# An encoder layer with routed experts on one core: GpSimd's order, paired tile transfers, scatters three to a slot, and expert tiles in every second slot

## The chip, the core and the metric

The kernel runs on one core of one Trainium2 chip. Engines are named as in the profile: PE is TensorE (PEld its weight load), DVE VectorE, ACT ScalarE, POOL GpSimd; SP is the sequencer that issues most DMAs. The metric is the device time of one execution in microseconds (us). Three runs of the kernel before have a median of 912.94 us (908.24 to 913.07).

## The reference

The input x has 64 sequences of 64 tokens with 128 features, the context the same shape. All arithmetic is float32. Cut to what matters:

```python
def _attn(q_in, k_in, v_in, wq, bq, wk, bk, wv, bv, wo, bo, causal):
    Q, K, V = ...                     # projections, 16 heads of 8
    scores = einsum('bqhd,bkhd->bhqk', Q, K) / sqrt(8)      # masked where causal
    return einsum('bhqk,bkhd->bqhd', softmax(scores), V).reshape(...) @ wo + bo

def _moe(x, rw, rb, w1, b1, w2, b2):                          # 8 experts, 128 -> 512 -> 128
    topw, topi = top_k(softmax(xf @ rw + rb), 2)
    combine = zeros.at[tokens, topi].add(softmax(topw))
    h = gelu(einsum('td,edf->etf', xf, w1) + b1)
    eo = einsum('etf,efd->etd', h, w2) + b2
    return einsum('etd,te->td', eo, combine)

x = _layernorm(x + _attn(x, x, x, ..., causal=True), ln1_g, ln1_b)
x = _layernorm(x + _attn(x, encoder_output, encoder_output, ..., causal=False), ln2_g, ln2_b)
x = _layernorm(x + _moe(x, ...), ln3_g, ln3_b)
```

## The kernel before

The 4096 tokens are 16 blocks of 256, each two tiles of 128 tokens. The program is one list of **slots** g, written out for every engine; each engine walks through the slots in order and does in slot g what stands there for it (the functions `slot(g)`), with semaphores between the engines. Slot g = 4t + s brings one attention **unit**, a tile of 128 tokens: for s = 0, 1 self attention of block t, for s = 2, 3 cross attention of block t - 2. A unit is spread over some seven slots: scores and row maxima in g, the two exponentials (the second, L749, gives the high parts) and the low parts (`probs_low`, shared by VectorE and GpSimd) in g + 1, the weighing in g + 2, output projection and residual in g + 3 (GpSimd's `spread` makes rstd there), VectorE's `norm` and GpSimd's `gain` in g + 4, the logits and the float16 halves of the result (`x2_high` on ScalarE, `x2_low` on GpSimd) in g + 5. Attention ends in slot 76.

The blocks are five **chunks** of 2, 3, 4, 4 and 3 blocks. When a chunk's units are done, VectorE routes it (slots 20, 32, 48, 64, 76 and the two behind each), GpSimd scatters its rows, sorted by expert, into a DRAM buffer `xs` (`scatter`, from slots 23, 35, 51, 67, 79, four indirect DMAs a slot), and the rows are worked off in **tiles** of 128 rows of one expert: 15, 19, 23, 23 and 19, together 99, numbered 0 to 98. TILE_SLOT says in which slot each stands. A tile needs its expert's weights (`load_tile_weights`, 512 KB, three tiles ahead, four buffers) and its rows (`load_tile_rows`, 64 KB, four tiles ahead, six buffers). PE turns the rows (`turn_tile`), multiplies up (`up`, 16 matmuls), ScalarE applies Gelu (L790), PE multiplies down (`down`, 9 matmuls), ScalarE copies y (`copy_y`) and SP stores it (`store_tile`). In each slot the first tile's step stands amid the attention work, further ones behind it: `for x in tiles[:1]: ...` and, at the end of the slot, `for x in tiles[1:]: ...`. In the slot before a chunk's first tile the chunk **opens**: SP issues three tiles' weights, waits for all scatters, and issues the first rows, and PE's last instruction of that slot turns them.

When a chunk's y is stored, GpSimd gathers for each block (a **group** f, at slot GROUP_SLOT[f]) the two picks of each token (`fetch_picks`, four indirect DMAs); VectorE sums and takes statistics two slots on (`gather_sum`), GpSimd makes rstd (`last_spread`, two slots on), VectorE normalizes (`final_norm`, three on) and GpSimd scales and stores to `out` (`last_gain`, three on). GpSimd's order in a slot is: x + bo, gain, x2_low, last_gain, last_spread, scatters, fetch_picks, probs_low, spread.

## Time and profile before

| what | value |
|---|---|
| median of 3 runs | 912.94 us |
| profiled execution: time, span | 903.71 us, 901.9 us |
| busy PE, PEld | 608.6 us (67%), 481.0 us (53%) |
| busy DVE, ACT, POOL | 475.6, 473.3, 388.2 us (53%, 52%, 43%) |
| granted clock of PE, mean | 0.851 of full speed |
| ACT_TABLE_LOAD | 92 of 1283 ns |
| POOL scatter L644, gather L658 | 64 of 1010 ns, 64 of 979 ns |
| POOL prob_lo L635, rstd L623, veps L621 | 979, 557, 224 ns each |
| POOL final_var_eps L664, frs L666 | 196, 717 ns each |
| DVE sums of picks with statistics (L1073, L1078, L1081, L1083) and final norm (L1092) | 12.5 + 12.3, 7.8, 2.5, 3.8 and 9.7 us for 16 groups |
| POOL waiting for x_hl (L629 on ACT L778) | 154.8 us in 32 times |
| PE waiting for a tile's rows (L1354 on xs) | 30.7 us in 5 times |

The first rows are shares of the whole span. Times "each" are means over all of a line's instructions, and an idle time in front of an instruction counts only where that engine holds up others. The kernel passes through stages of different kinds, so the rows further down are cut by stretches: attention alone (slots to 25), attention with tiles (26 to 71), tiles alone, and the end, in which GpSimd and VectorE finish the last chunk's blocks.

### The profile page before, as it was taken

How to read it: one execution, taken by the hardware profiler on the slowest of the kernel's cores; microseconds unless marked ns; L12 is line 12 of the kernel's file. 1: busy time of each engine (PE TensorE's matmuls, PEld its weight loads, DVE VectorE, ACT ScalarE, POOL GpSimd, SP SyncE). 2: the span in 40 equal slices, each digit the busy share in tenths (PEclk: the TensorE clock that was granted, in tenths of full speed). 3: DMA queues.
4: the chain of work that ended last, by engine and by line, in shares of the span. 5: the costliest groups of instructions: out<-in, count | busy, mean ns of one | idle time of the engine just before them, and what ended most of it. 6: DMA issues, size and time to landing. Idle time of an engine off the chain costs nothing. (4 is left out here: it accounts for less than half of the span.)

```text
span 901.9 us, 21537 instructions
## 1 busy us (share of the span) xinstructions
PE 608.6 (67%) x7898; PEld 481.0 (53%) x7898; DVE 475.6 (53%) x1319; ACT 473.3 (52%) x857; POOL 388.2 (43%) x611
## 2 busy tenths in 40 slices
PE   2677766666898785777877867787766766447800
PEld 1344444444776564665765646666555656446700
DVE  4468887575776754476785635665632144013021
ACT  1245454323899574686885856667626354123400
POOL 7133343235243461545235735354361466246064
PEclk9987897666999796898998879899976899778965
DMA  4625568235465425454554435535533566447710
GB/s 106 180 75 149 147 184 284 76 89 158 127 181 159 144 87 151 121 169 126 145 159 126 134 110 155 156 118 160 173 100 124 169 206 210 129 128 216 225 41 23
DMA packets 146024, 128.94 MB, mean 143 GB/s; under 512 B 14112, under 2 KB 127408, under 8 KB 145920
## 3 DMA queue, kind: packets, MB, share of 16 engines
q1 hardware_dynamic: 140864, 116.80, 43.7%
q0 software_dynamic: 5056, 10.76, 4.1%
q8 instruction: 64, 1.05, 0.5%
q14 instruction: 40, 0.33, 0.1%
HBM read 89.37 MB, written 40.24 MB: 144 GB/s over the span
## 5 line engine op out<-in xcount | busy, mean ns | idle before, releaser
L1384 PE MATMUL bank<-w_in,w_hl 128*128 128x128 f32 x792 | 126.9, 311 | 0.0
L921 DVE TENSOR_REDUCE row_max<-bank 128x16 bf16<-128x1024 f32 x64 | 78.2, 1222 | 87.0 <-PE bank L1266 78.1
L1384 PEld LDWEIGHTS bank<-w_in,w_hl 128*128 128x128 f32 x792 | 112.1, 219 | 0.4
L1314 PE MATMUL bank<-consts,o_n 128*128 128x64 f32 x256 | 47.1, 314 | 76.4 <-DVE o_n L940 64.4
L746 ACT ACTIVATE probT<-bank 128x1024 f32<-128x1024 f32 x64 | 65.5, 1024 | 60.0 <-PE bank L1290 34.5
L1373 PE MATMUL bank<-xT,w_in 128*128 128x128 f16 x1188 | 92.0, 231 | 4.1 <-issue 4.1
L658 POOL DMA_INDIRECT w_hl<-ys,pos x64 | 62.6, 979 | 72.5 <-DMA ys<-w_hl 54.5
L1314 PEld LDWEIGHTS bank<-consts,o_n 128*128 128x128 f32 x256 | 39.7, 220 | 90.2 <-issue 64.6
L790 ACT ACTIVATE w_hl<-bank 128x512 f32<-128x512 f32 x99 | 59.1, 597 | 54.7 <-PE bank L1373 34.6
L635 POOL TENSOR_TENSOR prob_lo<-probT,prob_hi 128x384 f16<-128x384 f32 x64 | 62.7, 979 | 51.2 <-ACT prob_hi L749 50.8
L1354 PE MATMUL bank<-ident_f,xs_tile 128*128 128x128 f16 x198 | 29.7, 235 | 79.9 <-ACT w_hl L798 39.2
L1373 PEld LDWEIGHTS bank<-xT,w_in 128*128 128x128 f16 x1188 | 78.9, 104 | 5.4 <-issue 5.4
L629 POOL TENSOR_TENSOR x_hl<-x_rows,x_hl 128x128 f16<-128x128 f32 x32 | 14.4, 451 | 154.8 <-ACT x_hl L778 154.8
L968 DVE TENSOR_SCALAR yn<-res,mv,rstd 128x128 f32<-128x128 f32 x64 | 25.7, 402 | 96.7 <-POOL rstd L623 96.2
L644 POOL DMA_INDIRECT xs<-x_hl,pos x64 | 64.6, 1010 | 18.8 <-issue 16.8
L914 DVE TENSOR_TENSOR prob_lo<-probT,prob_hi 128x640 f16<-128x640 f32 x64 | 57.1, 893 | 28.3 <-ACT prob_hi L749 28.3
L798 ACT ACTIVATE w_hl<-bank 128x128 f32<-128x128 f32 x99 | 27.3, 276 | 73.9 <-PE bank L1384 59.0
L1354 PEld LDWEIGHTS bank<-ident_f,xs_tile 128*128 128x128 f16 x198 | 12.5, 99 | 98.7 <-issue 66.7
L749 ACT ACTIVATE prob_hi<-bank 128x1024 f16<-128x1024 f32 x64 | 65.1, 1018 | 0.0
L783 ACT ACTIVATE xT<-bank 128x256 f16<-128x256 f16 x99 | 38.2, 386 | 46.7 <-PE bank L1354 43.4
L1290 PEld LDWEIGHTS bank<-q_st,k_all 128*64 128x64 f16 x2048 | 43.9, 125 | 34.4 <-issue 34.4
L1306 PE MATMUL bank<-v_hi,prob_hi 128*128 128x36 f16 x512 | 47.1, 181 | 20.4 <-issue 12.7
(149 smaller groups left out, 1606.4 us busy)
## 6 DMA issues: line engine op xcount, KB each, us to landing
...
k_all<-k_scr SPq DMA_DIRECT2D x128, 64.0 KB, 3.3
...
```

The lines of the kernel that those rows point to most:

```text
L635: pool.tensor_tensor(p_lo[u.buf][:, h, :], probT[u.buf][:, h, :], p_hi[u.buf][:, h, :], ALU.subtract).then_inc(lo_second[u.kind], 1)
L644: pool.indirect_dma_start(xs[c], bass.IndirectOffsetOnAxis(pos[c][:, k, t:t + 1], 0), x2_hl[:, n, :], None).then_inc(scattered[c], 16)
L658: pool.indirect_dma_start(got[f % 2][:, t, k, :], None, ys[c], bass.IndirectOffsetOnAxis(pos[c][:, k, n:n + 1], 0)).then_inc(got_in[f % 2] ...
L746: act.activation(probT[u.buf][:, :, :].rearrange("p h q -> p (h q)"), bank[:, KEYS:KEYS + 2, :].rearrange("p a n -> p (a n)"), ACT.Exp, sc ...
L749: act.activation(p_hi[u.buf][:, :, :].rearrange("p h q -> p (h q)"), bank[:, KEYS:KEYS + 2, :].rearrange("p a n -> p (a n)"), ACT.Exp, sca ...
L790: act.activation(hid[x.par][:, :, :].rearrange("p c t -> p (c t)"), bank[:, H_B, :], ACT.Gelu, scale=1 / W1_SCALE).then_inc(h_done, 1)
L914: dve.tensor_tensor(p_lo[u.buf][:, h, :], probT[u.buf][:, h, :], p_hi[u.buf][:, h, :], ALU.subtract).then_inc(lo_first[u.kind], 1)
L921: dve.reduce_max(row_max[u.buf][:, :], bank[:, SC:SC + 2, :].rearrange("p a (h k) -> p (a h) k", k=S), AX.X).then_inc(max_done[a], 1)
L1306: last = pe.matmul(bank[:, O_B, 36 * p:36 * p + 36], pt, v, start=k == 0, stop=k == 2, skip_group_check=True)
L1314: last = pe.matmul(turned_o[:, 64 * b:64 * b + 64], o_n[u.buf][:, b, :, :, :].rearrange("p c a d -> p (c a d)"), consts[:, C_DELTA:C_TRI], ...
L1373: last = pe.matmul(v[:, c * P:(c + 1) * P], w1_t[x.wb][:, i, c * P:(c + 1) * P], xT[x.par][:, j * P:(j + 1) * P], start=False, stop=True, ...
L1384: last = pe.matmul(expert_y, hid[x.par][:, c, :], w2_t[x.wb][:, c, :], start=False, stop=c == FC - 1, skip_group_check=True)
```

## The change

- `SCATTERS` is 3 a slot while attention runs, 8 behind it (before: 4).
- `TILE_SLOT`: while attention runs, a tile's slot is made odd (`g | 1`), so an even slot has no tile and an odd one two or three. The chunks' first tiles stand in slots 27, 41, 59, 75, 82 (before 26, 39, 56, 72, 83), so the chunks open in 26, 40, 58, 74 and 81.
- Groups of the first three chunks stand in every second slot: 42, 44; 60, 62, 64; 76, 78, 80, 82; then 83 to 86; 88, 89, 90 (before 40, 41; 57 to 59; 73 to 76; 84 to 87; 89 to 91).
- GpSimd's order in a slot is now: x + bo, gain, scatters, fetch_picks, last_spread, probs_low, spread, x2_low, last_gain; x2_low of a unit comes a slot later, last_spread three slots behind its fetch, last_gain five; VectorE's final_norm four. Small buffers of the final statistics are doubled.
- Rows and y of two tiles go in one DMA of 128 KB (`load_pair_rows`, `store_pair`; three buffers of pairs each). A pair is stored when the tile behind it is reached. The register read of a tile's weight row stands before the wait.

```diff
-SCATTERS = 4
+SCATTERS, LATE_SCATTERS = 3, 8
-WB, XB, YB = 4, 6, 4
+WB, XB, YB = 4, 3, 3
...
-        out += [g0 + i * n // TILES_OF[c] for i in range(TILES_OF[c])]
+        out += [g | 1 if (g := g0 + i * n // TILES_OF[c]) < ATTENTION_END else g for i in range(TILES_OF[c])]
...
-        g0 = max([TILE_SLOT[FIRST_TILE[c] + TILES_OF[c] - 1] + 2] + [out[-1] + 1 for _ in out[-1:]])
-        out += [g0 + i for i in range(CHUNK[c])]
+        step = 2 if MOE0[c] < ATTENTION_END - 4 else 1
+        g0 = max([TILE_SLOT[FIRST_TILE[c] + TILES_OF[c] - 1] + 1 + step] + [out[-1] + step for _ in out[-1:]])
+        out += [g0 + step * i for i in range(CHUNK[c])]
...
+                row = sp.value_load(tile_row[x.c][0:1, x.k:x.k + 1], min_val=0, max_val=(E - 1) * P)
                 if x.m >= WB:
                     sp.wait_ge(y_ready, x.m - WB + 1)
-                row = sp.value_load(tile_row[x.c][0:1, x.k:x.k + 1], min_val=0, max_val=(E - 1) * P)
...
+            def store_pair(x):
+
+                n = x.in_pair()
+                sp.wait_ge(y_done, x.m + n)
...
                 for x in tiles_in(g):
-                    if y := x.near(-2):
-                        store_tile(y)
-                    if y := x.near(XB - 2):
-                        load_tile_rows(y)
+                    if not x.half:
+                        if y := x.near(2 * XB - 2):
+                            load_pair_rows(y)
+                        if y := x.near(-2):
+                            store_pair(y)
                     if y := x.near(WB - 1):
                         load_tile_weights(y)
...
-                if (u := unit_at(g - 5)) and u.kind == CROSS:
-                    x2_low(u)
-                if (f := group_in(g - 3)) is not None:
-                    last_gain(f)
-                if (f := group_in(g - 2)) is not None:
-                    last_spread(f)
                 for c, n, k in scatters_at(g):
                     scatter(c, n, k)
                 if (f := group_in(g)) is not None:
                     fetch_picks(f)
+                if (f := group_in(g - 3)) is not None:
+                    last_spread(f)
                 if u := unit_at(g - 1):
                     probs_low(u)
                 if u := unit_at(g - 3):
                     spread(u)
+                if (u := unit_at(g - 6)) and u.kind == CROSS:
+                    x2_low(u)
+                if (f := group_in(g - 5)) is not None:
+                    last_gain(f)
...
-                if (f := group_in(g - 3)) is not None:
+                if (f := group_in(g - 4)) is not None:
                     final_norm(f)
```

How the instructions stand now, in three places. First GpSimd in slot 35, the first with scatters of the second chunk (yg and x_rows are the gain, x_hl is x2_low, xs the scatter). Before, the whole slot:

```order
L609 TENSOR_TENSOR yg<-yn,ln_g 128x128
L615 TENSOR_TENSOR x_rows<-yg,ln_b 128x128
L629 TENSOR_TENSOR x_hl<-x_rows,x_hl 128x128
L644 DMA xs<-x_hl,pos 2432x256 x4
L635 TENSOR_TENSOR prob_lo<-probT,prob_hi 128x384
L621 TENSOR_TENSOR veps<-mv,eps 128x1
L623 TENSOR_TENSOR rstd<-veps,minus_half 128x1
```

After, from the end of the gain in slot 35 to the end of slot 36:

```order
L640 TENSOR_TENSOR x_rows<-yg,ln_b 128x128
L669 DMA xs<-x_hl,pos 2432x256 x3
L660 TENSOR_TENSOR prob_lo<-probT,prob_hi 128x384
L646 TENSOR_TENSOR veps<-mv,eps 128x1
L648 TENSOR_TENSOR rstd<-veps,minus_half 128x1
L634 TENSOR_TENSOR yg<-yn,ln_g 128x128
L640 TENSOR_TENSOR x_rows<-yg,b_bo 128x128
L669 DMA xs<-x_hl,pos 2432x256 x3
L660 TENSOR_TENSOR prob_lo<-probT,prob_hi 128x384
L646 TENSOR_TENSOR veps<-mv,eps 128x1
L648 TENSOR_TENSOR rstd<-veps,minus_half 128x1
L654 TENSOR_TENSOR x_hl<-x_rows,x_hl 128x128
```

The scatters and the low part no longer have x_hl ahead of them: that unit's x_hl stands at the end of slot 36. Three scatters stand where four did.

Then ScalarE in attention with tiles (probT and prob_hi are the exponentials, w_hl<-bank 128x512 the Gelu, xT the copy of the turned rows). Before, one slot with a tile, up to the next one's exponentials:

```order
L746 ACT_TABLE_LOAD
L746 ACTIVATE probT<-bank 128x1024
L749 ACTIVATE prob_hi<-bank 128x1024
L783 ACTIVATE xT<-bank 128x256
L790 ACT_TABLE_LOAD
L790 ACTIVATE w_hl<-bank 128x512
L798 ACTIVATE w_hl<-bank 128x128
L725 ACTIVATE k_hl<-bank,bk 128x256
L737 ACTIVATE v_hi<-bank 64x2x16x8 x2
L778 ACTIVATE x_hl<-x_rows 128x128
L758 ACTIVATE oT<-bank 128x128
L772 ACTIVATE x_tile<-bank,ln_bc,ln_gc 128x128
```

After, from the exponentials of an even slot to the Gelu in the odd one behind it:

```order
L771 ACT_TABLE_LOAD
L771 ACTIVATE probT<-bank 128x1024
L774 ACTIVATE prob_hi<-bank 128x1024
L743 ACTIVATE inT<-bank 128x256 x2
L803 ACTIVATE x_hl<-x_rows 128x128
L783 ACTIVATE oT<-bank 128x128
L792 ACTIVATE x1T<-bank,ln_bc,ln_gc 128x128
L771 ACTIVATE probT<-bank 128x1024
L774 ACTIVATE prob_hi<-bank 128x1024
L808 ACTIVATE xT<-bank 128x256
L815 ACT_TABLE_LOAD
L815 ACTIVATE w_hl<-bank 128x512
```

Before, each slot has a table load ahead of the exponentials and one ahead of the Gelu; now the load for the exponentials stands in the even slot alone, the one for the Gelu in the odd. ACT_TABLE_LOAD stands 92 times in the program before and 58 times in this one.

Last GpSimd at the program's end, from the first gather of the last chunk's picks (w_hl<-ys,pos) on. Before:

```order
L658 DMA w_hl<-ys,pos 128x128 x4
L672 TENSOR_TENSOR w_hl<-w_hl,ln_g 128x256
L675 TENSOR_TENSOR w_hl<-w_hl,ln_b 128x256
L678 DMA out<-w_hl 128x2x128
L658 DMA w_hl<-ys,pos 128x128 x4
L664 TENSOR_TENSOR final_var_eps<-fmv,eps 128x2
L666 TENSOR_TENSOR frs<-final_var_eps,minus_half 128x2
L658 DMA w_hl<-ys,pos 128x128 x4
L672 TENSOR_TENSOR w_hl<-w_hl,ln_g 128x256
L675 TENSOR_TENSOR w_hl<-w_hl,ln_b 128x256
L678 DMA out<-w_hl 128x2x128
```

After:

```order
L683 DMA w_hl<-ys,pos 128x128 x4
L689 TENSOR_TENSOR final_var_eps<-fmv,eps 128x2
L691 TENSOR_TENSOR frs<-final_var_eps,minus_half 128x2
L697 TENSOR_TENSOR w_hl<-w_hl,ln_g 128x256
L700 TENSOR_TENSOR w_hl<-w_hl,ln_b 128x256
L703 DMA out<-w_hl 128x2x128
L683 DMA w_hl<-ys,pos 128x128 x4
L689 TENSOR_TENSOR final_var_eps<-fmv,eps 128x2
L691 TENSOR_TENSOR frs<-final_var_eps,minus_half 128x2
L697 TENSOR_TENSOR w_hl<-w_hl,ln_g 128x256
L700 TENSOR_TENSOR w_hl<-w_hl,ln_b 128x256
L703 DMA out<-w_hl 128x2x128
```

Behind the first gather there now stand a spread and a gain of the chunk before, and so behind the second one and, for the gain, the third. From there to the end come seven gains with stores to `out` and five spreads, where there were four and three.

## Rows read from the trace of the kernel before

**Rows 1.** Stretches: start:end length, busy us of each engine (instructions), PEclk, DMA share, GB/s

```profile
111.36:132.51 21.15, 13.55 (x228) 9.86 (x224) 17.70 (x45) 11.73 (x24) 9.64 (x19) 1.00 0.65 186
235.84:274.40 38.56, 34.47 (x553) 27.48 (x550) 29.22 (x74) 36.44 (x62) 15.04 (x28) 1.00 0.61 174
274.40:284.07 9.67, 8.11 (x115) 6.19 (x111) 5.06 (x16) 8.00 (x16) 3.60 (x8) 1.00 0.37 112
356.37:366.79 10.42, 9.17 (x142) 7.50 (x141) 6.63 (x17) 8.58 (x16) 2.92 (x6) 0.99 0.41 123
```

**Rows 2.** Timeline of ScalarE in slot 31: start us, us, engine, line, operation

```profile
264.32 1.28 ACT L746 ACT_TABLE_LOAD   x1
...
267.85 1.28 ACT L790 ACT_TABLE_LOAD   x1
269.14 0.60 ACT L790 ACTIVATE w_hl<-bank 128x512 f32<-128x512 f32 x1
```

**Rows 3.** Timeline of TensorE, end of slot 32 and start of 33; in brackets idle before, releaser

```profile
280.47 0.55 PE L1314 MATMUL bank<-consts,o_n 128*128 128x64 f32 x3 [0.37 <-ACT w_hl L798]
```

**Rows 4.** Timeline of GpSimd in slot 35

```profile
308.57 0.60 POOL L629 TENSOR_TENSOR x_hl<-x_rows,x_hl 128x128 f16<-128x128 f32 x1 [1.33 <-ACT x_hl L778]
...
315.37 0.57 POOL L623 TENSOR_TENSOR rstd<-veps,minus_half 128x1 f32<-128x1 f32 x1
```

**Rows 5.** Stretches between second exponentials of named slots

```profile
190.22:225.29 35.07, 24.71 (x249) 16.11 (x250) 19.95 (x54) 11.21 (x23) 18.41 (x28) 0.60 0.42 126
...
302.89:336.29 33.40, 26.05 (x335) 19.72 (x333) 19.28 (x56) 21.56 (x38) 20.93 (x30) 0.85 0.34 100
336.29:356.37 20.08, 9.56 (x104) 7.42 (x102) 7.33 (x17) 7.57 (x15) 4.12 (x8) 0.67 0.53 157
366.79:446.17 79.38, 62.58 (x894) 50.31 (x892) 52.91 (x139) 59.31 (x100) 37.83 (x64) 0.91 0.50 146
472.47:515.35 42.88, 34.45 (x451) 26.91 (x450) 25.59 (x71) 29.24 (x49) 28.54 (x39) 0.84 0.41 122
515.35:531.91 16.56, 9.43 (x103) 7.16 (x102) 6.37 (x17) 7.88 (x15) 3.81 (x8) 0.69 0.42 127
543.61:599.80 56.19, 42.18 (x568) 34.20 (x566) 36.32 (x100) 37.46 (x63) 27.30 (x44) 0.88 0.50 146
619.86:693.89 74.03, 49.54 (x599) 41.33 (x596) 30.34 (x101) 40.39 (x74) 29.69 (x44) 0.82 0.44 133
693.89:861.68 167.79, 109.36 (x1200) 100.03 (x1197) 36.57 (x150) 61.69 (x141) 71.50 (x93) 0.89 0.58 177
```

**Rows 6.** Timelines of SP's DMA queue and of TensorE in slot 38

```profile
340.42 2.64 SPq L487 DMA_DIRECT2D w_in<-w_scr  x3
...
348.46 0.40 PE L1354 MATMUL bank<-ident_f,xs_tile 128*128 128x128 f16 x2 [9.24 <-DMA xs_tile<-xs]
```

**Rows 7.** Timeline of ScalarE: Gelu (L790) of tiles 57, 79, 80, 88 and 89

```profile
696.50 0.60 ACT L790 ACTIVATE w_hl<-bank 128x512 f32<-128x512 f32 x1
...
783.84 0.60 ACT L790 ACTIVATE w_hl<-bank 128x512 f32<-128x512 f32 x1 [0.62 <-PE bank L1373]
...
797.26 0.60 ACT L790 ACTIVATE w_hl<-bank 128x512 f32<-128x512 f32 x1 [1.20 <-PE bank L1373]
...
829.77 0.60 ACT L790 ACTIVATE w_hl<-bank 128x512 f32<-128x512 f32 x1 [0.53 <-PE bank L1373]
...
832.41 0.60 ACT L790 ACTIVATE w_hl<-bank 128x512 f32<-128x512 f32 x1 [0.53 <-PE bank L1373]
```

**Rows 8.** Timeline of GpSimd at the program's end

```profile
861.68 1.05 POOL L658 DMA_INDIRECT w_hl<-ys,pos  x1 [30.29 <-DMA ys<-w_hl]
...
866.56 0.74 POOL L672 TENSOR_TENSOR w_hl<-w_hl,ln_g 128x256 f32<-128x256 f32 x1
...
868.40 0.81 POOL L678 DMA_DIRECT2D out<-w_hl  x1 [0.29 <-POOL w_hl L675]
...
891.13 0.76 POOL L678 DMA_DIRECT2D out<-w_hl  x1 [0.30 <-POOL w_hl L675]
```

More of the change, by code:

```diff
@@ L132, with scatters_in @@
 SCATTER = [r + 3 for r in ROUTE]
-MOE0 = [SCATTER[c] + -(-2 * NT[c] // SCATTERS) + 1 for c in range(CHUNKS)]
 ATTENTION_END = last_cross(CHUNKS - 1) + 6
+def scatters_in(slot):
+    return SCATTERS if slot < ATTENTION_END else LATE_SCATTERS
+MOE0 = [SCATTER[c] + -(-2 * NT[c] // scatters_in(SCATTER[c])) + 1 for c in range(CHUNKS)]
 TAIL_RATE = 4
@@ L159, in __init__, with in_pair @@
         self.first, self.last = self.k == 0, self.k == TILES_OF[self.c] - 1
-        self.par, self.wb, self.xb, self.yb = m % 2, m % WB, m % XB, m % YB
+        self.par, self.wb = m % 2, m % WB
+        self.half = self.k % 2
+        self.pair = FIRST_PAIR[self.c] + self.k // 2
+        self.xb, self.yb = self.pair % XB, self.pair % YB
+    def in_pair(self):
+        return 1 if self.last else 2
     def near(self, d):
         return Tile(self.m + d) if 0 <= self.k + d < TILES_OF[self.c] else None
+LAST_OF = {Tile(m).pair: m for m in range(NMOE)}
 def tiles_in(slot):
@@ L399, in uses_of @@
         def uses_of(k, c):
-            return sum(m % YB == k for m in range(FIRST_TILE[c] + TILES_OF[c]))
+            return sum(p % YB == k for p in range((FIRST_PAIR + [Tile(NMOE - 1).pair + 1])[c + 1]))
         @blk.sync
@@ L549, in slot @@
                     sp.wait_ge(cleared, 16 * CHUNKS)
-                    for d in range(XB - 2):
-                        load_tile_rows(x.near(d))
+                    for d in range(XB - 1):
+                        load_pair_rows(x.near(2 * d))
             load_tokens(SELF, Block(0))
@@ L1347, in turn_tile @@
             def turn_tile(x):
[L1349 removed]
+                pe.wait_ge(xs_in[x.xb], 16 * (x.pair // XB + 1))
                 if x.m == 0:
```

60 lines of the change are left out of this document (32 added, 28 removed).

## Prediction

> **What bounds the kernel now.** I read the stretches first, then ScalarE's timeline in a quiet place, then GpSimd's in a disturbed one. The second exponential (L749) runs once a slot, so its starts give every slot's length; the stretches are cut at them. In three quiet slots without an expert tile a slot takes 21.15 / 3 = 7.05 us, with VectorE busy 17.7 of 21.15: the round of maxima, low parts, o_n and back through TensorE. In five quiet slots with one tile each it takes 38.56 / 5 = 7.7 us, with ScalarE busy 36.4 of 38.56; a slot with two takes 9.7 or, where more projections stand in it, 10.4 [rows 1]. ScalarE is full there because each slot loads the table of Exp and the table of Gelu, 1.28 us each [rows 2]. So one tile hides nearly whole (+0.65), a second hardly: it stands at the slot's end, PE begins the next slot's L1314 only at 280.47, after the copy of the second tile's result, some 2.5 us late [rows 3].
>
> That is the quiet pace. Slots 26 to 63 hold 46 tiles, eight slots with two; at 7.7 and 10.0 (between 9.7 and 10.4) they would need 30 x 7.7 + 8 x 10.0 = 311 us. Three things stand on top. In slots with scatters GpSimd waits for ScalarE's x_hl, then issues four indirect transfers of 1.3 us, and only then makes the low probabilities and rstd, on which VectorE's normalization waits [rows 4]. In slots that gather picks the same happens. And where a chunk opens, PE stands for its first rows [rows 6]. The rest is read from the stretches [rows 5]. Slots 35 to 37 take 33.4 us, 10.3 over the pace; slots 51 to 54 take 42.9, 12.1 over; slots 23 to 25 take 35.1. The picks cost 79.4 - 63.9 = 15.5 and 56.2 - 43.1 = 13.1. The openings in slots 38 and 55 take 20.1 and 16.6, so 12.4 and 8.9 over.
>
> **The change part by part.**
>
> *GpSimd's order and three scatters a slot.* x2_low no longer stands before the scatters and the low probabilities. GpSimd's round in a scatter slot becomes normalization 0.5, gain 1.0, three scatters 3.8, low part 0.95, rstd 1.0, x2_low 0.45 and the handovers: about 8.0 (durations from the table above). In a slot without tiles that is 1 us over 7.05; in one with two or three tiles it hides. Slots 23 to 56 have 13 scatter slots after the change, 8 of them without tiles: 8 us, where slots 23, 24, 35 to 37 and 51 to 54 now lose 9.7 + 10.3 + 12.1 = 32 (slots 23 and 24 begin at 190.22 and take 23.85 of the 35.07). **-24.**
>
> *Picks in every second slot.* Five fetches fall into slots without tiles: four gathers of 1.27 make GpSimd's round about 9, +2 each; five sums with their normalization, 48.6 / 16 = 3.0 us each by the table above, fall on VectorE, which has 1.15 us a slot free there: +1.9 each. Some 19 for 28.6 now. **-10.**
>
> *Tiles in the second of two slots.* ScalarE saves 34 table loads of 92, 34 x 1.28 = 43.5 us of work. What that is worth is read from the pace: a pair now costs 2 x 7.7 = 15.4, and then 7.05 + 10.0 = 17.05, as ScalarE stops being the bound and the serial second tile takes its place. Slots 26 to 63 become 19 x 7.05 + 14 x 10.0 + 5 x 12.7 (three tiles, one more 2.64) = 337.5 for 311. **+26.** The bounds: if every load saved were time, -43.5; if the two-tile slots take 10.4 and the empty ones are no shorter than a slot with one tile, 14 x 0.4 + 19 x 0.65 = 18 more, +44. I take the middle of the measured slots.
>
> On the table switch the row says that Gelu starts at 269.14, right behind a load of 1.28 us from 267.85 [rows 2]. The Trainium skill (ScalarE: Activation LUTs, What ACT_TABLE_LOAD costs) gives 1283 ns for the load, which the row confirms, and 1380 ns of drain on top, which it does not show. By the page 34 switches would be worth 90 us and the advice to group by table set would decide the case; by the rows they are worth 43.5 at most.
>
> *Openings.* The first chunk now opens in slot 26, the second in 40, the third in 58. SP there must send and fetch q and k (26, 58), or wait for PE's turn of the tokens and then send k (40), before it issues three weight tiles and the rows; rows reach PE 8 us after the first weight issue (340.42 to 348.46) [rows 6]. In slot 38 the first weight issue stands 4.1 us behind the second exponentials (340.42 to 336.29) and the slot takes 20.1, with 2.1 of the old chunk's last tile in it: 18, less 7.7 is 10, which I take for 58. In 26 the slot before has no tile, so the exponentials come earlier and SP's sends do not: I put 4 more; in 40 PE's turn of the tokens stands before the send: 3 more. Both are choices between 0 and the 8 us that the load takes. That is 14 + 13 + 10 = 37, for 4.2 (slot 25, 35.07 - 23.85 - 7.05) + 12.4 + 8.9 = 25.5 now. Two paired loads for four shorten SP's issue by 0.9 us. **+9** after rounding down for that.
>
> The paired transfers do nothing else: the rows' four issues take 1.77 us and PE's waits for rows are those of the openings. The Trainium skill (DMA: Bandwidth & Descriptors, Rules for kernel authors) says to coalesce many small transfers into large ones; its fixed cost of about 2 us (stated for the GpSimd path) would, as an estimate, save 4 us at each of five openings, and the time would be 922. The row has the rows land behind three weight tiles of 512 KB, which pairing leaves alone.
>
> *Slots 64 to 71*, 74.0 us now [rows 5]: -3, since the fourth opening leaves them and scatters stand three to a slot.
>
> Attention together: -24 - 10 + 26 + 9 - 3 = **-2.**
>
> *The fourth chunk.* It now opens in slot 74 with no attention left to cover it. Now its first Gelu runs 2.6 us after the last exponentials (693.89 to 696.50). After the change come two tiles of the third chunk in slot 73 and its last down projection in 74, some 12 us, then an opening as bare as the fifth chunk's is now: 797.26 - 783.84 = 13.4 us from Gelu to Gelu [rows 7]. That is 25 for 2.6: +22. The 42 tiles behind it need 2.64 each at best (829.77 to 832.41), 111 us of the 167.8 [rows 5, 7]; less of attention's finish stands between them, -4. **+18.**
>
> *The end.* Now GpSimd waits until 861.68 for the last rows of y and then issues three groups' gathers (5.0 each), four gains with their stores (2.7 each, 866.56 to the end of the store at 869.21) and three spreads (1.0 each, by the table above), and issues the last store at 891.13 [rows 8]: 30.2 us. After the change the last three gains of chunk four and two of its spreads stand behind the first gather of chunk five in GpSimd's order. They have been ready for long, but GpSimd sits in the wait. That is 3 x 2.7 + 2 x 1.0 = 10 us; normalizations that wait for out stores just issued (landing some 2 us later, an estimate from the 8.0 us that three weight tiles and a tile's rows take [rows 6]) add about 3. **+13.**
>
> The sum is -2 + 18 + 13 = +29 us. On the profiled execution, 903.7 us (span 901.9), that is 933; that execution is 9.2 us under the median of the three runs, 912.9. The measured time should stand to the median: **942 us**.
>
> **The rivals.**
>
> *Faster (14%).* ScalarE's saved loads come through as time: the tile's second step overlaps the following empty slot, since that slot's PE has 7.6 of 21.15 us free [rows 1]. A pair then costs 14.1 in place of 17.05, 19 pairs give -56, and the sum is about -27: 886 us. For it: ScalarE is nearly full now. Against it: the two-tile slots in the trace are already longer by the whole second step.
>
> *No change (9%).* Fewer stalls keep PE's clock up: it is granted 0.60 in slots 23 to 25 and 0.67 in the opening slot, against 1.00 where it is quiet [rows 1, 5]. If that gives 10 us, and the bare opening costs half of what I say and the sum for pairs 10 less, I am at 913.
>
> *Much slower (12%).* Loads of weights wait behind indirect transfers, which now come in the same slots as nothing else, and 3-tile slots ask 1.5 MB at once; each of the nine three-tile slots then loses 2 us more, and the empty slots take 7.7: +18 and +12, 972 us.
>
> *The change does not do what it says*: pairing and spreading move no bound and GpSimd's wait for x_hl was idle anyway. Without the -24 the time is 966; it shares the 12% of the case before.
>
> **How the numbers follow.** My forecast, 925 to 960, has 65%. The range reaches from 908, which takes in most of the unchanged case, to 964; it leaves out the faster case and half of the slowest. What a measurement can tell from no change is 0.5%, 4.6 us. Faster 14% and a little of the lower edge, 0.15; same 0.09; slower 0.76.
>
> **What would show it.** Right: 58 table loads; no GpSimd wait for x_hl before scatters; starts of the second exponentials alternating near 7 and 10; a PE stall of 7 to 10 us for rows behind slots 26, 40, 58 and 74; about 43 us from GpSimd's first gather of the last chunk to its last store. Wrong: pairs near 15 us, or the fourth chunk's gains done before that gather. The attention part up to the last exponentials should end at 692, within 15 us; if it ends at 660, the term for the pairs is wrong.

## The result, and the profile after

The changed kernel takes 966.4 us (median of 4 runs, 966.2 to 972.9) against 910.6 (903.6 to 913.1): a ratio of 1.066, 95% interval 1.061 to 1.070. It is slower, as forecast, but by 56 us and not by 29. The profiled execution takes 966.2 us with a span of 964.4, 62.5 over the span before. Cut at the second exponentials (now L774), with the kernel of e1 beside it, which is the changed one with its tiles one to a slot. Slots 26 to 63 hold 46 tiles before, 43 after and in e1:

| stretch, us | before | after | e1 | forecast for the change |
|---|---|---|---|---|
| up to slot 23 | 190.2 | 199.0 | 191.2 | 0 |
| slots 23 to 25 | 35.1 | 28.4 | 27.6 | |
| slots 26 to 63 | 394.6 | 427.1 | 375.9 | with the row above and below: -2 |
| slots 64 to 71 | 74.0 | 73.0 | 70.6 | |
| last exponentials to last copy of y | 165.1 | 181.6 | 182.8 | +18 |
| last copy of y to last store | 32.1 | 44.4 | 44.4 | +13 |

The stretches of after, in the form of [rows 1, 5]: slots 10 to 19; 23 to 25; 26 to 63; then slots 28, 30, 31 (two tiles), 32, 33 (three tiles), and 28 to 31 together.

```profile
core 0: us, PE busy (x) PEld busy (x) DVE busy (x) ACT busy (x) POOL busy (x), PEclk, DMA share, GB/s
83.28:165.31 82.03, 57.24 (x775) 39.30 (x771) 62.90 (x145) 38.41 (x74) 28.03 (x49) 0.79 0.61 184
199.04:227.43 28.39, 19.70 (x268) 13.12 (x269) 20.37 (x55) 10.81 (x22) 18.22 (x27) 0.76 0.26 75
227.43:654.50 427.07, 307.64 (x4242) 236.25 (x4238) 250.00 (x660) 240.79 (x439) 173.45 (x278) 0.86 0.43 129
256.71:265.68 8.97, 5.93 (x60) 3.36 (x58) 5.03 (x13) 3.40 (x8) 2.99 (x6) 0.70 0.33 95
277.30:284.11 6.81, 4.67 (x56) 3.11 (x55) 5.18 (x16) 3.64 (x8) 3.21 (x5) 0.76 0.57 164
284.11:295.47 11.36, 9.95 (x162) 8.42 (x161) 7.38 (x17) 8.87 (x18) 2.57 (x5) 1.00 0.47 146
295.47:304.45 8.98, 5.93 (x59) 3.36 (x57) 5.32 (x15) 3.41 (x9) 2.99 (x6) 0.63 0.33 96
304.45:320.17 15.72, 12.60 (x201) 10.77 (x202) 9.57 (x31) 12.24 (x21) 3.65 (x7) 0.99 0.39 114
256.71:295.47 38.76, 31.52 (x440) 23.97 (x437) 24.11 (x59) 24.20 (x46) 12.42 (x23) 0.87 0.43 131
```

The last second exponential starts at 727.5 us; the forecast had 692, within 15.

ScalarE did save what the change was made for: it is busy 240.8 us in slots 26 to 63 (284.2 before, 280.4 in e1), and the whole program has 58 table loads. But none of the three prices of the forecast for a pair stands. A quiet slot with two tiles takes 11.4 us (10.0 forecast), one with three 15.1 to 15.7 (12.7), and a slot without tiles 5.9 to 9.0 (7.05), mostly at a granted clock of 0.63 to 0.76. Slots 28 to 31 hold four tiles in 38.8 us.

What fills a two-tile slot is in ScalarE's and PE's timeline of slot 31. The second tile's xT copy (289.74) stands behind k_hl, v_hi and x_hl; PE waits 1.04 us for it, and o_n, which VectorE has ready at 288.5, is turned (L1341) only at 291.80.

```profile
287.37 0.28 ACT L823 ACTIVATE w_hl<-bank 128x128 f32<-128x128 f32 x1
288.25 0.47 ACT L750 ACTIVATE k_hl<-bank,bk 128x256 f16<-128x256 f32 x1 [0.60 <-PE bank L1274]
288.62 0.76 ACT L762 ACTIVATE v_hi<-bank 64x256 f16<-64x256 f32 x2
289.40 0.31 ACT L803 ACTIVATE x_hl<-x_rows 128x128 f16<-128x128 f32 x1
289.74 0.38 ACT L808 ACTIVATE xT<-bank 128x256 f16<-128x256 f16 x1
290.02 0.59 ACT L815 ACTIVATE w_hl<-bank 128x512 f32<-128x512 f32 x1
```

```profile
288.39 0.83 PE L1400 MATMUL bank<-xT,w_in 128*128 128x128 f16 x12
290.26 0.22 PE L1408 MATMUL bank<-b_all,chosen_biases 128*128 128x128 f16 x1 [1.04 <-ACT xT L808]
290.32 1.11 PE L1411 MATMUL bank<-w_in,w_hl 128*128 128x128 f32 x8
291.80 0.66 PE L1341 MATMUL bank<-consts,o_n 128*128 128x64 f32 x4 [0.37 <-ACT w_hl L823]
```

Slot 47 has two tiles in both kernels, the same copies between them and a granted clock of 1.00. It takes 10.7 us before and 11.2 after, where a slot without a tile stands in front of it. PE's share in it is larger: before, PE has weighed just as the second exponential starts; after, it weighs 1.0 to 1.6 us behind that start. First before, then after:

```profile
435.48:446.22 10.74, 8.52 (x114) 6.70 (x111) 5.73 (x17) 8.76 (x18) 2.92 (x6) 1.00 0.62 175
```

```profile
462.11:473.27 11.16, 9.75 (x160) 8.22 (x158) 7.64 (x20) 8.76 (x17) 7.16 (x12) 1.00 0.45 128
```

The tail is as forecast. The fourth chunk's first Gelu runs 26.0 us behind the last exponentials (25 forecast, 2.6 before), and PE waited for its rows; ScalarE's rows:

```profile
727.54 1.02 ACT L774 ACTIVATE prob_hi<-bank 128x1024 f16<-128x1024 f32 x1
...
753.53 0.60 ACT L815 ACTIVATE w_hl<-bank 128x512 f32<-128x512 f32 x1 [1.35 <-PE bank L1400]
```

So is the end: GpSimd's timeline from the first gather of the last chunk to the last store, 41.8 us (29.5 before [rows 8]). Spreads and gains of chunk four stand between the gathers (here the first such pair).

```profile
911.83 1.03 POOL L683 DMA_INDIRECT w_hl<-ys,pos  x1 [28.92 <-DMA ys<-w_hl]
...
916.66 0.20 POOL L689 TENSOR_TENSOR final_var_eps<-fmv,eps 128x2 f32<-128x2 f32 x1
916.94 0.72 POOL L691 TENSOR_TENSOR frs<-final_var_eps,minus_half 128x2 f32<-128x2 f32 x1
917.65 0.71 POOL L697 TENSOR_TENSOR w_hl<-w_hl,ln_g 128x256 f32<-128x256 f32 x1
...
933.18 1.04 POOL L683 DMA_INDIRECT w_hl<-ys,pos  x1 [4.18 <-DVE w_hl L1100]
...
953.59 0.75 POOL L703 DMA_DIRECT2D out<-w_hl  x1 [0.29 <-POOL w_hl L700]
```

### The profile page after: what moved, and what is told of

Read it like the earlier page. It is cut to its first block and busy times, and to the rows that moved or that the text cites. A ratio compares the mean times of both kernels' runs of the same rounds, so it can differ in the third digit from the quotient of the medians.

```text
span 964.4 us, 21371 instructions
## 1 busy us (share of the span) xinstructions
PE 619.0 (64%) x7898; PEld 480.0 (50%) x7898; DVE 482.3 (50%) x1319; ACT 433.1 (45%) x823; POOL 395.5 (41%) x611
## 5 line engine op out<-in xcount | busy, mean ns | idle before, releaser
L946 DVE TENSOR_REDUCE row_max<-bank 128x16 bf16<-128x1024 f32 x64 | 78.3, 1224 | 190.2 <-PE bank L1293 162.4
L660 POOL TENSOR_TENSOR prob_lo<-probT,prob_hi 128x384 f16<-128x384 f32 x64 | 67.4, 1053 | 157.6 <-ACT prob_hi L774 156.8
L1341 PE MATMUL bank<-consts,o_n 128*128 128x64 f32 x256 | 51.1, 334 | 109.4 <-DVE o_n L965 90.9
L1411 PE MATMUL bank<-w_in,w_hl 128*128 128x128 f32 x792 | 115.8, 291 | 0.0
L1341 PEld LDWEIGHTS bank<-consts,o_n 128*128 128x128 f32 x256 | 42.3, 235 | 122.7 <-issue 105.8
L1411 PEld LDWEIGHTS bank<-w_in,w_hl 128*128 128x128 f32 x792 | 101.6, 200 | 0.7 <-issue 0.2
L646 POOL TENSOR_TENSOR veps<-mv,eps 128x1 f32<-128x1 f32 x64 | 14.4, 226 | 176.7 <-DVE mv L984 176.7
L939 DVE TENSOR_TENSOR prob_lo<-probT,prob_hi 128x640 f16<-128x640 f32 x64 | 67.0, 1047 | 31.8 <-ACT prob_hi L774 31.7
L1400 PEld LDWEIGHTS bank<-xT,w_in 128*128 128x128 f16 x1188 | 78.4, 104 | 0.0
L1119 DVE TENSOR_SCALAR w_hl<-w_hl,fmv,frs 128x128 f32<-128x128 f32 x32 | 13.4, 460 | 123.1 <-POOL frs L691 58.7
L783 ACT ACTIVATE oT<-bank 128x128 f32<-128x128 f32 x64 | 17.8, 278 | 113.5 <-PE bank L1354 88.6
L1317 PEld LDWEIGHTS bank<-q_st,k_all 128*64 128x64 f16 x2048 | 47.7, 132 | 39.5 <-issue 39.5
L774 ACT ACTIVATE prob_hi<-bank 128x1024 f16<-128x1024 f32 x64 | 65.1, 1017 | 0.0
L1305 PE MATMUL bank<-max_diag,consts_bf 128*128 128x512 bf16 x128 | 51.4, 491 | 8.4 <-DVE max_diag L951 8.4
```

The source lines that it names most:

```text
L660: pool.tensor_tensor(p_lo[u.buf][:, h, :], probT[u.buf][:, h, :], p_hi[u.buf][:, h, :], ALU.subtract).then_inc(lo_second[u.kind], 1)
L774: act.activation(p_hi[u.buf][:, :, :].rearrange("p h q -> p (h q)"), bank[:, KEYS:KEYS + 2, :].rearrange("p a n -> p (a n)"), ACT.Exp, sca ...
L939: dve.tensor_tensor(p_lo[u.buf][:, h, :], probT[u.buf][:, h, :], p_hi[u.buf][:, h, :], ALU.subtract).then_inc(lo_first[u.kind], 1)
L946: dve.reduce_max(row_max[u.buf][:, :], bank[:, SC:SC + 2, :].rearrange("p a (h k) -> p (a h) k", k=S), AX.X).then_inc(max_done[a], 1)
L1305: pe.matmul(bank[:, KEYS + n, :], ones_bf, max_diag[u.buf][:, 4 * n:4 * n + 4, :, :].rearrange("p a q c -> p a c q"), start=True, stop=True)
L1341: last = pe.matmul(turned_o[:, 64 * b:64 * b + 64], o_n[u.buf][:, b, :, :, :].rearrange("p c a d -> p (c a d)"), consts[:, C_DELTA:C_TRI], ...
```

## The experiments

All results, as ratios to the kernel before on the same chip. Runs of different lines stood partly on different chips (medians of before: 907.1 to 914.2), so ratios are compared, not medians. Ratios move from chip to chip too: the same kernel has 1.055 in e14 and 1.064 in e18. A difference of 1% between runs on different chips is therefore not settled by the table. The stretch is slots 26 to 63 of the profiled execution; it holds 46 tiles in the kernel before, e2 and e4, 41 in e3, 44 in e10 and e12, and 43 in the others. The same code differs there from profile to profile: 422.7 to 428.8 us for the changed kernel with either kind of transfer, 375.9 and 370.0 in e1 and e7.

| run | median us | ratio (95% interval) | 26 to 63 |
|---|---|---|---|
| changed kernel | 966.4 | 1.066 (1.061 to 1.070) | 427.1 |
| e1 tiles one to a slot | 909.5 | 0.999 (0.995 to 1.004) | 375.9 |
| e2 before, tiles in odd slots | 958.8 | 1.049 (1.041 to 1.057) | 436.1 |
| e3 changed, even slots | 979.6 | 1.072 (1.064 to 1.081) | 415.7 |
| e5 changed, filler | 951.9 | 1.051 (1.045 to 1.056) | 409.3 |
| e6 changed, second step earlier | 961.7 | 1.061 (1.056 to 1.065) | 422.0 |
| e4 before, x2_low late | 912.6 | 1.001 (0.996 to 1.006) | 399.9 |
| e8 before, three scatters | 915.2 | none (runs of 903.4 to 921.6 us) | 395.1 |
| e9 e1, single transfers | 898.0 | 0.989 (0.985 to 0.992) | 368.4 |
| e15 e9, groups each slot | 917.6 | 1.006 (1.002 to 1.009) | 377.6 |
| e16 e9, x2_low early | 913.9 | 1.002 (0.997 to 1.006) | 376.3 |
| e7 e1, gains first | 902.9 | 0.997 (0.994 to 0.999) | 370.0 |
| e10 e7, chunk 4 opens sooner | 910.3 | 1.010 (1.005 to 1.016) | 383.9 |
| e11 e7, early filler | 893.4 | 0.985 (0.983 to 0.988) | 375.3 |
| e12 e10, early filler | 902.2 | 0.997 (0.994 to 1.001) | 382.4 |
| e13 e9, gains first, early filler | 894.2 | 0.979 (0.973 to 0.984) | 371.7 |
| e14 changed, single transfers | 967.9 | 1.055 (1.049 to 1.060) | 427.6 |
| e17 changed kernel again | 970.3 | 1.065 (1.058 to 1.072) | 428.8 |
| e18 e14 again, beside e17 | 965.8 | 1.064 (1.058 to 1.069) | 422.7 |

### What the pairs of slots cost: e1 and e2

```diff
-        out += [g | 1 if (g := g0 + i * n // TILES_OF[c]) < ATTENTION_END else g for i in range(TILES_OF[c])]
+        out += [g0 + i * n // TILES_OF[c] for i in range(TILES_OF[c])]
```

> The changed kernel with its tiles spread one to a slot as before; order of GpSimd, paired transfers, three scatters and groups in every second slot stay. Theory P (the pairs of slots cost, because a second tile's step stands serially at the end of an odd slot): slots 26 to 63, 427.1 us in the changed kernel, fall by 26 to 35 us, the last second exponential comes near 695, and the whole is 930 to 940 us. Rival O (the new order of GpSimd and the openings cost, the pairs are free): 26 to 63 fall by less than 8 us and the whole stays over 955. In both, slots 1 to 22 stay as long as in the changed kernel (start of slot 23 at 199).

e2 is the same line the other way round, in the kernel before.

> The kernel before with one edit: a tile's slot is made odd while attention runs. Theory P: two-tile slots take 11 to 11.5 us, empty ones 7 to 7.5, so slots 26 to 63 (394.6 us before) grow by 20 to 35 and the whole is 930 to 945 us. Rival (the 34 saved table loads come through as time): 870 to 900 us. Rival O (the pairs are free): 905 to 918 us.

The pairs of slots are the whole slowdown: without them the changed kernel is level with the one before, and alone they cost 1.049. In slots 26 to 63 they cost 51.2 us from e1 and 41.5 from the kernel before, more than either theory had put down, and both medians fell outside every range given. Slot 23 of e1 starts at 191.2 and not at 199. Slots 28 to 31 of e1, four tiles one to a slot, at full clock, take 31.1 us where the changed kernel takes 38.8:

```profile
247.58:278.64 31.06, 27.92 (x455) 22.46 (x453) 25.25 (x60) 28.84 (x50) 13.49 (x23) 1.00 0.56 164
```

### Where the second step stands: e3 and e6

e3 rounds the slot up to an even one (`g + g % 2` for `g | 1`).

> The changed kernel with its tiles in even slots in place of odd ones (a slot's number rounded up). Theory K (the odd slots are the bad hosts: in them ScalarE copies key and value, 0.47 and 0.76 us, between the two Gelus, and the two-tile slot takes 11.4 us where an even one took 9.7): two-tile slots of s = 0 take 9.7 to 10.2 us, and the whole is 945 to 958 us. Rival (which of the two slots makes no difference; the second step costs the same anywhere): 962 to 972 us.

e6 moves the second tile's step, on both engines:

```diff
+                early = 2 if g < ATTENTION_END else 1
-                for x in tiles[:1]:
+                for x in tiles[:early]:
                     tile_step(x)
...
+                for x in tiles[1:early]:
+                    ...
                 if s == 0 and (sa.exists() or ca.exists()):
```

> The changed kernel with the second tile's step placed ahead of the projections on TensorE and ahead of their copies on ScalarE, while attention runs. Theory K (the second step's xT copy waits behind ScalarE's 0.94 to 1.23 us of key, query and value copies, and its matmuls behind 1.0 us of projections, and the two-tile slot takes 11.4 for it): two-tile slots take 10 to 10.4 us, 19 slots give 20 us, the whole is 942 to 952 us. Rival (the work is the same and only its order differs): 960 to 970 us.

Neither run bears K out in size. In e3 quiet two-tile slots of s = 0 take 10.7 and 10.3 us (9.7 to 10.2 expected), those of s = 2 11.4 and 10.5, and the whole missed both ranges. Its chunks open a slot later and more of its groups stand at the end (last copy of y to last store: 53.2 us); e3 doesn't separate the two. In e6 slot 31 takes 11.0 instead of 11.4, and the whole stays in the rival's range: a gain of 0.4 to 0.5%, which the intervals don't tell from none. The work has only changed places: now ScalarE waits 0.45 and 0.53 us inside the second step, which nothing covers, and k_hl and v_hi stand ahead of oT instead.

```profile
282.65 0.38 ACT L808 ACTIVATE xT<-bank 128x256 f16<-128x256 f16 x1 [0.45 <-PE bank L1382]
283.56 0.60 ACT L815 ACTIVATE w_hl<-bank 128x512 f32<-128x512 f32 x1 [0.53 <-PE bank L1401]
...
285.44 0.47 ACT L750 ACTIVATE k_hl<-bank,bk 128x256 f16<-128x256 f32 x1 [0.60 <-PE bank L1275]
285.82 0.76 ACT L762 ACTIVATE v_hi<-bank 64x256 f16<-64x256 f32 x2
286.60 0.31 ACT L803 ACTIVATE x_hl<-x_rows 128x128 f16<-128x128 f32 x1
286.94 0.28 ACT L783 ACTIVATE oT<-bank 128x128 f32<-128x128 f32 x1
```

### What the empty slots cost: e5

```diff
+            def filler(g, n):
+                if MOE0[0] <= g < ATTENTION_END and not tiles_in(g):
+                    ...
+                    for k in range(n):
+                        pe.matmul(bank[:, H_B, (k % 4) * P:(k % 4 + 1) * P], ident_h[:, :], ident_h[:, :], ...)
```

> The changed kernel with filler work on TensorE: in every slot without a tile, 12 and at its end 16 matmuls of 128 columns into the bank that holds Gelu's input, whose result nobody reads. Theory G (the slots without a tile are long because TensorE's granted clock falls in them, 0.70 on the mean of 19 such slots against 0.98 in the two-tile slots): their granted clock rises to 0.9 or more, the quiet ones go from about 7.9 to 7.1 us, and the whole falls by 8 to 15 us, 951 to 958 us. Rival S (the serial second and third step are all of it): the 28 matmuls cost or are hidden, the whole is 964 to 985 us.

Adding work made the kernel 1.4% faster, by the ratios of e5 and e17 too, which stood on one chip; the whole is in theory G's range. Slots 28, 30 and 32 take 7.2, 5.9 and 7.2 us for 9.0, 6.8 and 9.0, at a granted clock of 1.00; over the 19 slots without a tile the clock goes from 0.70 to 0.85 and the mean length from 9.7 to 8.5.

```profile
254.16:261.38 7.22, 5.70 (x100) 4.25 (x99) 5.04 (x13) 3.42 (x9) 2.98 (x6) 1.00 0.31 89
271.90:277.76 5.86, 5.29 (x99) 4.43 (x96) 5.58 (x16) 3.68 (x8) 2.69 (x4) 1.00 0.55 154
288.59:295.81 7.22, 5.70 (x100) 4.25 (x99) 5.33 (x15) 3.42 (x9) 2.98 (x6) 1.00 0.32 90
```

So of the 51 us some 18 are the clock (427.1 - 409.3): a mean of 0.70 says that PE ran its share of the attention round partly at 1.2 GHz and not at 2.4, and with the filler slots 26 to 63 as a whole have the granted clock of e1, 0.91. This also shows what a quiet pair costs at full clock. Slots 28 to 31, two pairs, take 34.4 us, 17.2 a pair, for the 17.05 of the forecast and 19.4 in the changed kernel; slots 32 and 33, none and three tiles, take 22.4 for 19.75:

```profile
254.16:288.59 34.43, 30.39 (x491) 24.97 (x491) 24.61 (x59) 24.01 (x45) 12.61 (x23) 1.00 0.50 146
288.59:310.98 22.39, 17.75 (x286) 14.64 (x286) 15.52 (x46) 15.64 (x28) 6.63 (x13) 1.00 0.41 125
```

The other 33 us I put down to the second and third steps behind which the round waits, as in slot 31; that is what is left over, and no run takes them away.

### GpSimd's order, scatters and groups: e4, e8, e15, e16

e4: in the kernel before, x2_low moves to the end of the slot, at `g - 6`. e8: in the kernel before, `SCATTERS, LATE_SCATTERS = 3, 8`. e15: e9 with `step = 1`. e16: e9 with x2_low at `g - 5` ahead of the scatters.

> The kernel before with one edit: GpSimd's x2_low comes a slot later and last in the slot. Theory X (the 8.8 us that slots 5 to 22 lose in the changed kernel come from this: GpSimd's low probabilities now always run beside VectorE's max_diag, 1.36 for 0.69 us, and TensorE's granted clock falls to 0.7): slot 23 starts at 197 to 200; the scatter slots gain about 10, so the whole is 905 to 915 us. Rival C (the loss of slots 5 to 22 is a clock that differs from run to run): slot 23 starts at 189 to 192 and the whole is 893 to 905 us.

> The kernel before with one edit: three scatters a slot while attention runs and eight behind it, so that the chunks open in slots 26, 39, 57, 73, 81. Theory A (of the 29 us that slots 23 to 71 gain in e1, the three scatters a slot give 15 to 20): the last second exponential at 674 to 681 for 693.9, the tail 15 to 18 longer because the fourth chunk opens bare: 905 to 915 us. Rival (GpSimd's order gives them; three scatters alone leave slots 23 to 71 within 6 us): 920 to 932 us.

> e9 with the groups of picks in slots that follow each other (41, 42; 59, 60, 61; 75 to 78). Theory (my term for picks: a group every second slot is worth 10 us in slots 26 to 63): those slots take 376 to 382 us for 368.4, the whole is 905 to 912 us. Rival (the spacing moves nothing): 895 to 902 us.

> e9 with x2_low a slot earlier and ahead of the scatters again, as before the change. Theory (GpSimd's order is worth most of what is left of the 24 us term, in the scatter slots): slots 23 to 63 longer by 8 to 16 us, the whole 905 to 914 us. Rival (e4 and e8 say that neither the order nor the three scatters alone does anything; then the final statistics' staging does it): 895 to 902 us.

Alone, neither brings a gain of the whole. The late x2_low leaves slots 23 to 71 where they were (504.2 us for 503.7). The three scatters shorten them by 6.9 us, 5.3 of it in slots 23 to 25, and make the last exponentials to the last y 15.1 us longer, since the fourth chunk then opens bare; e8's two theories had 15 to 20 and under 6 for the first part, so neither is right.

Taken out of e9, the spacing of the groups costs 1.7% in all (9.2 us in slots 26 to 63) and the place of x2_low 1.3% (7.9 us there, 3.7 in slots 23 to 25), but e15 and e16 ran on another chip than e9. On their own chip stands e13, which has the same code in slots 27 to 63 and takes 371.7 us in 26 to 63: against it the spacing is worth 5.9 us there and the place of x2_low 4.6, no more than e1 and e7 differ by. In the whole, e15 and e16 are 2.8 and 2.4% behind e13. Its early filler (0.9 to 1.3%, e12 and e11) and its gains ahead of the fetch (0.3% by the ratios of e7 and e1, 0.9% by the 8 us of the end) account for 1.2 to 2.2% of that, which leaves, as an estimate, 0.6 to 1.6% for the spacing and 0.2 to 1.2% for x2_low. So both probably help, and x2_low's worth is hardly clear of noise. e16 fell in its theory's range, e15 (917.6) over both of its ranges. What the three scatters bring among the other parts, no run shows.

Theory X holds in part (e4's slot 23 starts at 194.8 us, between the two ranges). Slots 10 to 19 hold no tile and no scatter in any kernel. Over all profiled executions they take 75.2 to 78.4 us in the four kernels with x2_low early and 78.0 to 83.5 in the thirteen others without early filler: some 4 us for the place, as much again from run to run. Both go with the clock: before, and e7 (x2_low late):

```profile
81.03:156.23 75.20, 51.01 (x776) 36.43 (x772) 61.85 (x145) 38.43 (x73) 27.68 (x49) 0.89 0.67 200
```

```profile
83.26:166.78 83.52, 59.52 (x776) 40.84 (x771) 62.88 (x145) 38.42 (x73) 28.28 (x50) 0.76 0.62 185
```

What x2_low's move does there is seen in slots 15, 16 and 19, where x2_low stood in front: GpSimd's prob_lo no longer waits for ScalarE's x_hl and starts 2 to 4 us sooner. In slot 15 it then starts beside VectorE's max_diag, which takes 1.36 us. In the kernel before it took 0.69 there with GpSimd waiting (the 1.36 is found in the kernel before too, in slot 18, so it comes from the meeting and not from the new order alone). First after, VectorE and GpSimd, then before:

```profile
126.53 1.36 DVE L951 TENSOR_TENSOR max_diag<-consts_bf,row_max 128x1024 bf16<-128x1024 bf16 x1
...
126.43 0.91 POOL L660 TENSOR_TENSOR prob_lo<-probT,prob_hi 128x384 f16<-128x384 f32 x1 [1.23 <-ACT prob_hi L774]
```

```profile
119.68 0.69 DVE L926 TENSOR_TENSOR max_diag<-consts_bf,row_max 128x1024 bf16<-128x1024 bf16 x1
...
121.83 0.91 POOL L635 TENSOR_TENSOR prob_lo<-probT,prob_hi 128x384 f16<-128x384 f32 x1
```

The Trainium skill (SBUF — State Buffer, Who interferes with whom) says that a VectorE instruction with two SBUF inputs and a GpSimd instruction that reads SBUF block each other for a whole instruction. The rows nearly agree: prob_lo starts first, and max_diag ends 0.55 us behind its end, where alone it takes 0.69.

### The transfers: e9, e14, e17, e18

```diff
-WB, XB, YB = 4, 3, 3
+WB, XB, YB = 4, 6, 4
-        self.half = self.k % 2
-        self.pair = FIRST_PAIR[self.c] + self.k // 2
+        self.half = 0
+        self.pair = m
```

> The kernel of e1 with rows and y of each tile in a transfer of their own again. Theory (pairing moves nothing, since rows are waited for only behind an opening's weights): 905 to 914 us, slots 26 to 63 within 5 us of e1's 375.9. Rival (pairing is worth what the skill's rule on coalescing gives, or SP's shorter list is what made slots 26 to 63 fast): 918 to 930 us.

> The changed kernel with one transfer a tile for rows and y; its tiles stay in odd slots. Theory Q (pairing itself costs about 10 us, all of it at the five openings: the last but one y store of a chunk waits for the second y of its pair ahead of the next chunk's weights in SP's order, and the first rows are 128 KB): 953 to 960 us, the first Gelus of chunks four and five 2 to 4 us nearer to the tile before. Rival (e9's gain came from something that one tile a slot brings, or is the spread between chips): 963 to 970 us.

> The changed kernel once more, so that it stands on the same chip as e18: 962 to 974 us. Its slots 1 to 22 are the second look at the early loss: theory C (a granted clock that differs from run to run) lets slot 23 start anywhere from 190 to 200, a cost of the change would put it at 199 again.

> The kernel of e14, beside e17. If pairing costs 1% in the changed kernel, as the ratios to before say (1.0656 and 1.0547, taken on different chips), this is 8 to 11 us under e17. If the medians of e14 and of the changed kernel (967.9 and 966.4) tell it rightly, within 3 us of e17.

Across chips single transfers looked 1% faster twice (e9, e14). On one chip the changed kernel with pairs has 1.065 and without 1.064: no difference that can be told, and e18 is 4.5 us under e17, between its two cases; e14 fell in its rival's range. The openings differ by little: slot 58 takes 14.9 and 14.9 us in e14 and e18 for 17.3 and 16.8, the fifth chunk's first Gelu comes 14.2 and 14.2 us behind the last of the fourth for 15.9 and 16.2; the fourth chunk's goes the other way (17.7 and 18.2 for 16.6 and 17.0). The four openings behind the first, from a chunk's last Gelu to the next one's first, add up to 89.3 and 88.9 us with pairs and 85.7 and 86.6 without.

With one tile a slot theory Q holds. The same sum is 77.4, 77.6, 79.1, 77.8 and 78.1 us in the five kernels with paired transfers (e1, e7, e10, e11, e12) and 68.1, 67.1, 67.5 and 67.3 in the four with single ones (e9, e13, e15, e16): 10 us, on several chips. SP's queue shows where they go, here at the fifth opening. In e1 the last y store but one waits for the second y of its pair, and the new chunk's first weights are issued at 774.24, 2.5 us behind the last Gelu (771.78); in e13 at 768.03, 0.5 us behind it (767.55). First e1, then e13:

```profile
768.54 4.93 SPq L521 DMA_DIRECT2D ys<-w_hl  x2
774.24 2.58 SPq L507 DMA_DIRECT2D w_in<-w_scr  x3
```

```profile
764.31 2.96 SPq L521 DMA_DIRECT2D ys<-w_hl  x2
768.03 2.55 SPq L507 DMA_DIRECT2D w_in<-w_scr  x3
```

So e9's 1% over e1, which was outside both of its ranges, has a cause in the traces, though no two kernels that differ in this alone with one tile a slot were timed on one chip. The coalescing rule of the Trainium skill (DMA: Bandwidth & Descriptors, Rules for kernel authors) would, as the forecast worked it out, have given a gain at each opening; none is there.

### The end, the fourth chunk, and a faster kernel: e7, e10 to e13

e7, in GpSimd's slot:

```diff
+                if g > ATTENTION_END:
+                    if (f := group_in(g - 5)) is not None:
+                        last_gain(f)
+                    if (f := group_in(g - 3)) is not None:
+                        last_spread(f)
                 for c, n, k in scatters_at(g):
```

> The kernel of e1 (the changed one with one tile a slot) with last_gain and last_spread ahead of the fetch in the slots behind attention. Theory E (three gains and two spreads of the fourth chunk, 10 us, stand behind the first gather of the last chunk): from that gather to the last store 29 to 33 us in place of 41.7, the whole is 897 to 900 us. Rival (the end is bound by the gathers' landing, and the order of the gains only moves): over 906 us.

From the last chunk's first gather to the last store 34.2 us for 41.7; last copy of y to last store 36.3 for 44.4. Theory E holds for 8 of the 12 us: one gain and one spread of the fourth chunk now stand ahead of that gather (3.7 us), and GpSimd's wait of 4.2 us ahead of the third group's gathers is gone. The rest is the distance in slots: the fourth chunk's last three groups stand in 84, 85 and 86, and their gains, five slots behind, come after the first gather, in slot 88, in any order within a slot. The median, 902.9 us, lies between the two ranges.

e10: four scatters a slot from slot 64. e11: e7 with the filler in slots 5 to 26. e12: both. e13: e9 with e7's order and e11's filler.

> The kernel of e7 with four scatters a slot for the fourth chunk, which then opens in slot 71 in place of 73 (its tiles from 72, the third chunk's up to 71). Theory T (the 17.7 us that the tail lost is the fourth chunk's bare opening): from the last second exponential to the last y 166 to 172 us for 184.7; slots 64 to 71 longer by 3 to 6; the whole 888 to 894 us for 902.9. Rival (the opening costs the same inside attention as behind it): 899 to 906 us.

> The kernel of e7 with the filler of e5 (12 and 16 matmuls of 128 columns a slot, whose result nobody reads) in slots 5 to 26, before any tile. Theory G (there too the granted clock, which went 0.67 to 1.00 from slot to slot and run to run, sets the pace): slot 23 starts at 180 to 188 for 190 to 199, the whole is 890 to 898 us. Rival (those slots are VectorE's round and the extra work lies in TensorE's way): 902 to 912 us.

> The edits of e10 and e11 together. If both theories hold they add up: 874 to 886 us. If filler does not help, as e10.

> e9 (one tile a slot, single transfers) with e7's gains ahead of the fetch and e11's filler in slots 5 to 26. If the three gains add up: 907 less 10 (single transfers), 8 (gains) and 8 (filler), 878 to 888 us. If the filler or the end only moves idle time once the transfers are single: 889 to 898 us.

e10: the tail is 17.7 us shorter than in e7, as theory T has it (167.0 for 184.7), and attention 24 us longer, 14 in slots 64 to 71 and 14 in slots 26 to 63, less 4 in the early slots; the whole, 910.3 us, is over both ranges. The 14 us in slots 26 to 63 aren't the opening's: 10 of them stand in slots 59 to 63, where the third chunk's tiles must be done two slots sooner (slots 59 and 61 have two and take 12.9 and 12.5 us, for one and 7.9 and 8.0 in e7). So the run shows that bringing the opening forward cost more than it saved, and not what an opening alone costs inside attention. Early filler gives 1.1% (e11 to e7, on different chips) and 1.3% (e12 to e10, on one chip; 0.9% by the medians): slots 10 to 19 take 73.6 us at a granted clock of 1.00. e11 fell in theory G's range. e12 (902.2) missed both of its ranges, and e13 (894.2) fell in its second one, so the parts don't add up.

```profile
80.34:153.98 73.64, 59.97 (x1065) 48.41 (x1062) 64.27 (x145) 38.42 (x74) 28.27 (x49) 1.00 0.65 193
```

e11 and e13 beat both kernels, by 1.5% and 2.1% against the kernel before. Which of them is the faster isn't settled by the times, since they stood on different chips.

## Why the forecast came out as it did

*Tiles in the second of two slots, +26.* This is the step that failed: +51 (427.1 - 375.9), outside its upper bound of 44. The two stretches that the forecast compared don't hold the same number of tiles, 46 at one a slot for 311 us and 43 in pairs for 337.5. With the forecast's own prices e1's 43 tiles (31 slots with one, 6 with two, one empty) take 306, so the pairs should have cost +32 and not +26, and 51 came.

What went wrong first is the clock, for which the sum had no term. "Empty, 7.05" was read from slots that stand in a row at a granted clock of 1.00 [rows 1]; in quiet slots between two with two tiles it is 0.63 to 0.86, and giving it back takes 18 us off (e5). At full clock a quiet pair takes 17.2 us: there the price of 17.05 was right. Second, "one more, 2.64" was read from tiles behind attention, where steps overlap; a slot with three tiles takes 3.7 to 4.3 us more than a quiet one with two, and 15.2 in all even at full clock (e5, slot 33), for 12.7. "Two tiles, 10.0" was the middle of a slot with s = 0 (9.7) and one with s = 3 (10.4) [rows 1], and all new two-tile slots are odd: those with s = 3 have 1.23 us of copies between the Gelus and took 11.2 to 13.1, apart from slot 27 (10.5), and of those with s = 1, six of the fourteen, there was no row.

The forecast's terms for slots 26 to 63 add up to 395 us (337.5, some 5 for scatters and 16 for picks in slots without a tile, 37 for openings); 427.1 came. By the means of all these slots, two tiles take 11.9 us (14 slots), three 15.3 (5), none 7.9 outside the openings (16): 26 + 13 + 14 us over the prices, of which those 21 had been allowed for.

*GpSimd's order and scatters -24, picks -10, openings +9, slots 64 to 71 -3, together -28.* e1 has these without the pairs: slots 23 to 71 are shorter by 7.5 + 18.7 + 3.4 = 29.6 us, some 5 of which are the three tiles fewer in slots 26 to 63. The sum is right within a few us, its split isn't. The openings are right in the changed kernel (18.7 + 21.4 + 17.3 us, less three empty slots, is 35 for 37). By the lengths over the pace, e1's scatter slots (23 to 25, 35 to 38, 51 to 56) lose 23 us for 32 before, a gain of 9 and not 24; its slots behind the fetches (41 to 49, 59 to 63) lose 9 for 28.6, a gain of 20 and not 10. That these errors nearly cancel is luck, and that the parts add up isn't shown, since alone e4 gives nothing and e8 6.9 us.

*The fourth chunk, +18:* measured +16.5, and +17.7 in e1. e8, which only has the three scatters, lost 15.1 there, so the cause, a bare opening, is shown apart from the rest. *The end, +13:* +12.3. Both of its parts are in the rows: three gains and two spreads, and a wait of 4.18 us ahead of the third group's gathers, for a sum that stands on VectorE behind a normalization, which starts only 2.4 us after the out store at 928.19 was issued.

*Slots up to 23, 0:* +8.8 in this profile, of which some 4 are the change's (x2_low) and the rest differs from run to run, 191.2 to 199.2 for kernels with the same code there. The forecast had no term for it.

*The rivals.* "Faster" took the saved table loads for time. They were saved (39.6 us of ScalarE's time from e1 to the changed kernel), and PE and the serial step bound the pair. "No change" had the clock as its mechanism and its sign wrong: over slots 26 to 63 it is 0.86 after and 0.89 before. "Much slower" gave 972 with 2 us more for each three-tile slot and 7.7 for empty ones, which is about what came, by another cause: PE's waits in slots 26 to 63 name no weights, only rows at the three openings. "The change does not do what it says" gave 966 us, which is the number that was measured, and by luck: e1 shows that the parts without the pairs were worth what the forecast had them at.
